# Projections as split float32r products, and a half burst inside a score pair of the attention loop

## The reference, cut to what matters

```python
xn = _layernorm(x)                       # x: 4 x 512 tokens of 256 numbers
q = xn @ Wq.T; k = xn @ Wk.T; v = xn @ Wv.T
scores = jnp.einsum('bsqhd,bthd->bqhst', qh, kh) * scale   # 4 query groups, 8 heads of 8
a_dot = jnp.einsum('bqhst,bthd->bsqhd', jax.nn.softmax(scores), vh)
a_mem = sigma_q @ memory / (sigma_q @ memory_norm)         # sigma_q = elu(q)
out = x + (a_dot * (1 - w) + a_mem * w) + moe(xn)          # moe: shared MLP + 8 experts, top 2
```

## Time and profile before

| what | value |
|---|---|
| median of 3 runs | 735.35 us (734.99 to 736.04) |
| the profiled execution | 736.27 us, of which its span is 734.4 us |
| PE busy | 711.4 us (97%) |
| DVE busy | 577.1 us (79%) |
| ACT busy | 491.1 us (67%) |
| stage 1, up to the first router matmul | 0 to 34.31 us |
| attention, first to last step's first score | 143.3 to 447.5 us |

### The profile page before, as it was taken

How to read it: one execution, slowest core, us unless ns; L and a number is a source line. 1 busy time by engine, 2 the same in 40 slices (tenths; PEclk the granted TensorE clock), 3 DMA queues, 4 the chain that set the end, 5 groups by cost and what they waited for, 6 DMA issues and landing times.

```text
span 734.4 us, 16311 instructions
## 1 busy us (share of the span) xinstructions
PE 711.4 (97%) x5018; PEld 390.0 (53%) x5019; DVE 577.1 (79%) x784; ACT 491.1 (67%) x886; POOL 137.8 (19%) x298
## 2 busy tenths in 40 slices
PE   8999999899999999999999999899999999999998
PEld 3456544622222222222222223688888888888887
DVE  6276488899999999999999982577777878766755
ACT  2472600289999999999999897656566665656332
POOL 1000000666642222111222220100000000005750
PEclk9999999999999999999999999999999999999999
DMA  9829100167521111011111361051111111122431
GB/s 307 283 73 339 51 0 1 34 194 256 181 66 33 33 34 34 30 25 29 33 33 33 117 227 58 16 172 43 57 50 50 50 50 57 43 101 80 136 109 43
DMA packets 50002, 65.41 MB, mean 89 GB/s; under 512 B 8216, under 2 KB 42928, under 8 KB 49968
## 3 DMA queue, kind: packets, MB, share of 16 engines
q1 hardware_dynamic: 37232, 39.92, 17.1%
q10 hardware_dynamic: 9664, 16.66, 6.9%
q0 software_dynamic: 3072, 8.39, 3.6%
HBM read 40.15 MB, written 24.38 MB: 88 GB/s over the span
## 4 chain that ended last, share of the span: by engine, by line
PE 85%; ACT 7%; issue 3%; DVE 3%; POOL 1%; ACTq 1%; DVEq 0%; POOLq 0%
PE ps L1401 16%; PE ps L1432 14%; PE ps L1456 11%; PE ps L1502 9%; PE ps L1279 7%; PE ps L1536 6%; ACT att L752 5%; PE ps L1304 5%; PE ps L1271 3%; PE ps L1551 3%; PE ps L1493 2%; PE ps L1237 2%; ACT o_sb L711 1%; PE ps L1386 1%; PE ps L1414 1%
## 5 line engine op out<-in xcount | busy, mean ns | idle before, releaser
L1025 DVE TENSOR_REDUCE smax<-ps 128x2 f32<-128x1024 f32 x256 | 296.3, 1215 | 20.8 <-PE ps L1304 19.6
L752 ACT ACTIVATE att<-ps 128x512 f32<-128x512 f32 x512 | 274.2, 596 | 32.8 <-PE ps L1456 23.4
L1401 PE MATMUL ps<-att,v_head 128*32 128x256 f32 x2048 | 164.0, 392 | 6.5 <-ACT o_sb L711 6.1
L1456 PE MATMUL ps<-att 51*128 51x512 bf16 x512 | 158.4, 384 | 3.0 <-ACT att L752 1.7
L1304 PE MATMUL ps<-att 48*128 48x512 bf16 x512 | 155.4, 385 | 1.4 <-DVE smax L1025 1.4
L1432 PE MATMUL ps<-att_r 128*128 128x512 f32 x456 | 118.7, 409 | 2.8 <-DVE att_r L1086 2.8
L1082 DVE TENSOR_TENSOR att_r<-big,att_r 128x1024 fp32r<-128x1024 f32 x76 | 89.7, 1221 | 24.2 <-ACT att_r L732 24.2
L1432 PEld LDWEIGHTS ps<-att_r 128*128 128x128 f32 x456 | 86.2, 190 | 21.4 <-DVE att_r L1086 3.3
L1456 PEld LDWEIGHTS ps<-att 51*128 51x128 bf16 x512 | 35.5, 93 | 110.6 <-DVE smax L1025 40.0
L1401 PEld LDWEIGHTS ps<-att,v_head 128*32 128x32 f32 x2048 | 40.5, 108 | 98.2 <-issue 52.5
L732 ACT ACTIVATE att_r<-big 128x1024 fp32r x74 | 74.3, 1052 | 19.0 <-issue 19.0
(11 more groups left out here) (167 smaller groups left out, 702.9 us busy)
## 6 DMA issues: line engine op xcount, KB each, us to landing
big<-w ACTq DMA_DIRECT2D x8, 1024.0 KB
q_stacks<-big SPq DMA_DIRECT2D x12, 512.0 KB
att<-q_stacks SPq DMA_DIRECT2D x64, 96.0 KB
slot_x<-zeros SPq DMA_DIRECT2D x1, 4992.0 KB, 17.1
e_x<-slot_x SPq DMA_DIRECT2D x39, 128.0 KB, 2.0
slot_y<-xn SPq DMA_DIRECT2D x39, 128.0 KB, 1.7
big<-w ACTq DMA_DIRECT2D x8, 512.0 KB
att<-k_stacks SPq DMA_DIRECT2D x64, 48.0 KB
```

Source lines behind the costliest of these rows:

```text
L752: act.activation(probs[:, t % 2, g, :], ps[:, RING[turn_of(u) % 3], :], ACT.Exp, scale=SCALE)\
L1025: dve.reduce_max(smax[:, s % 2, :].rearrange("p (half v) -> p half v", half=2)[:, :, v], ps[:, bank:bank + 2, :], X_AXIS).then_inc(max_don ...
L1401: last = pe.matmul(ps[32 * g:32 * (g + 1), 6, queries], v_head[:, s % 2, t, :], probs[:, t % 2, g, queries], start=s % 2 == 0 and t == 0 a ...
L1456: pe.matmul(ps[:, RING[turn % 3], :], k_st[s][rows, P * t:P * (t + 1)], q_st[s][rows, g, :], start=True, stop=True).then_inc(scores_ready, 1)
```

## The change

In stage 1 each projection becomes three float32r products that are summed in PSUM: high part of the weights times high part of x, low part of the weights times high part of x, and (as `rest`) high part of the weights times low part of x. ACT makes the high parts by copying (the weights once, x from PSUM by `round_xT`), POOL takes the low parts of the weights by two subtractions, DVE those of x by two subtractions a group (`rest_of_xT`). ACT's work is put in another order: one projection result is copied first, then the rounding, then the square root, then the other results, then `copy_xT`. SP waits for the projection weights before it issues the loads of x for groups 2 and 3. Four warm-up matmuls fall away. In stage 3 the half burst that followed pair 2 and the turn of the maxima move into the middle of pair 3, between its two score matmuls; `MAX_AT` goes from 6 to 7 with them, and so does ACT's negation.

```diff
--- before.py
+++ after.py
@@ -154,6 +154,11 @@
         kc = [big[0:DKV, 18432 + 1024 * n:18432 + 1024 * (n + 1)].bitcast(BF16) for n in range(3)]
         wq_sb = big[:, 21504:22016].rearrange("p (k n) -> p k n", k=KD)
         wkv_sb = big[:, 22016:22272].rearrange("p (k n) -> p k n", k=KD)
+
+
+        p_hi, p_lo = [[split[:, 4096 + 2048 * a + 1024 * n:5120 + 2048 * a + 1024 * n]
+                       .rearrange("p (k n) -> p k n", k=KD) for a in range(2)] for n in range(2)]
+        pw_hi, pw_lo = [split[:, 8192 + 768 * n:8960 + 768 * n].rearrange("p (k n) -> p k n", k=KD) for n in range(2)]
         mtmp = big[:, 4096:6144].rearrange("p (a d) -> p a d", a=8)
 
         w1_sb = big[:, 0:16384].rearrange("p (e k n) -> p e k n", e=E, k=KD)
@@ -223,6 +228,10 @@
         xn_ready = sem("xn_ready")
         xT_in_psum = sem("xT_in_psum")
         xT_copied = sem("xT_copied")
+        pw_hi_ready = sem("pw_hi_ready")
+        pw_lo_ready = sem("pw_lo_ready")
+        p_hi_ready = sem("p_hi_ready")
+        p_lo_ready = sem("p_lo_ready")
         lT_in_psum = sem("lT_in_psum")
         lT_copied = sem("lT_copied")
         logits_in_psum = sem("logits_in_psum")
@@ -317,7 +326,7 @@
 
 
         RING = (4, 5, 7)
-        TURNS, MAX_AT, OUT_AT = 18, 6, 13
+        TURNS, MAX_AT, OUT_AT = 18, 7, 13
 
         LAST_OUT = 7
 
@@ -341,7 +350,7 @@
             for j in range(TILES // 2 * 2 - 2, TILES + 2):
                 tile(j, j // 2, j % 2)
 
-        WARM = 18
+        WARM = 14
         FIRST = 2 * NF
         LAST = 2 * NF
 
@@ -359,6 +368,8 @@
             for c in (0, 2):
                 sp.dma_start(acc[:, c, :], x_rows[P * c:P * (c + 1), :]).then_inc(x_first[c], 16)
             for n in range(1, 4):
+                if n == 2:
+                    sp.wait_ge(proj_loaded, 48)
                 sp.dma_start(acc[:, 4 * n:4 * n + 4, :],
                              x_rows[512 * n:512 * (n + 1), :].rearrange("(c p) d -> p c d", p=P))\
                   .then_inc(x_loaded[n - 1], 16)
@@ -517,6 +528,12 @@
                         out=slot_x, out_offset=bass.IndirectOffsetOnAxis(ap=slot[:, n:n + 1], axis=0),
                         in_=xn[:, n % NT, :], in_offset=None).then_inc(scattered, 16)
 
+            pool.wait_ge(pw_hi_ready, 1)
+            pool.tensor_tensor(pw_lo[:, :, 0:2 * P], wq_sb, pw_hi[:, :, 0:2 * P], ALU.subtract)\
+                .then_inc(pw_lo_ready, 1)
+            pool.wait_ge(pw_hi_ready, 2)
+            pool.tensor_tensor(pw_lo[:, :, 2 * P:3 * P], wkv_sb, pw_hi[:, :, 2 * P:3 * P], ALU.subtract)\
+                .then_inc(pw_lo_ready, 1)
             pool.wait_ge(v_copied, 2)
 
             def stage_v(i, b, h, s):
@@ -626,6 +643,7 @@
 
             def copy_xT(n):
                 act.wait_ge(xT_in_psum, n + 1)
+                act.wait_ge(p_lo_ready, n + 1)
                 act.activation(xnT[:, n % 2, 512 * (n // 2):512 * (n // 2 + 1)], ps[:, n % 4, :], ACT.Copy)\
                    .then_inc(xT_copied, 1)
 
@@ -639,15 +657,30 @@
                     ins = act.activation(qf[:, part - 1, 512 * n:512 * (n + 1)], ps[:, 4 + u % 4, :], ACT.Copy)
                 ins.then_inc(qk_copied, 1)
 
+            def round_xT(n):
+
+                act.wait_ge(xT_in_psum, n + 1)
+                if n >= 4:
+                    act.wait_ge(qk_in_psum, 3 * (n // 2 - 1))
+                act.activation(p_hi[n // 2 % 2][:, n % 2, :], ps[:, n % 4, :], ACT.Copy).then_inc(p_hi_ready, 1)
+
             sqrt_var(0)
+            act.wait_ge(proj_loaded, 48)
+            act.activation(pw_hi[:, :, 0:2 * P], wq_sb, ACT.Copy).then_inc(pw_hi_ready, 1)
+            act.activation(pw_hi[:, :, 2 * P:3 * P], wkv_sb, ACT.Copy).then_inc(pw_hi_ready, 1)
             for n in range(4):
+
+                done = range(*UNITS[n - 1]) if n > 0 else ()
+                for u in done[:1]:
+                    copy_qk(u)
+                round_xT(2 * n)
+                round_xT(2 * n + 1)
+                if n < 3:
+                    sqrt_var(n + 1)
+                for u in done[1:]:
+                    copy_qk(u)
                 copy_xT(2 * n)
                 copy_xT(2 * n + 1)
-                if n < 3:
-                    sqrt_var(n + 1)
-                if n > 0:
-                    for u in range(*UNITS[n - 1]):
-                        copy_qk(u)
             for u in range(*UNITS[3]):
                 copy_qk(u)
             act.wait_ge(lT_in_psum, 1)
@@ -868,6 +901,14 @@
                 dve.wait_ge(dve_step, count[0])
 
 
+            def rest_of_xT(n):
+                for m in (2 * n, 2 * n + 1):
+                    dve.wait_ge(p_hi_ready, m + 1)
+                    if n >= 2:
+                        dve.wait_ge(qk_in_psum, 3 * (n - 1))
+                    dve.tensor_tensor(p_lo[n % 2][:, m % 2, :], ps[:, m % 4, :], p_hi[n % 2][:, m % 2, :],
+                                      ALU.subtract).then_inc(p_lo_ready, 1)
+
             for n in range(4):
                 tiles = range(4 * n, 4 * n + 4)
                 part = slice(4 * n, 4 * n + 4)
@@ -882,6 +923,8 @@
                     last = dve.bn_aggr(meanvar[:, c, :], stats[:, c, :])
                 link(last)
                 dve.tensor_scalar_add(meanvar[:, part, 1], meanvar[:, part, 1], EPS).then_inc(var_ready, 1)
+                if n > 0:
+                    rest_of_xT(n - 1)
                 dve.wait_ge(sd_ready, n + 1)
                 link(dve.reciprocal(rstd[:, part], sd[:, part]))
 
@@ -892,6 +935,7 @@
                 for c in tiles:
                     dve.tensor_scalar(xn[:, c, :], acc[:, c, :], meanvar[:, c, 0:1], rstd[:, c:c + 1],
                                       ALU.subtract, ALU.mult).then_inc(xn_ready, 1)
+            rest_of_xT(3)
 
 
             dve.wait_ge(logits_in_psum, 1)
@@ -1224,27 +1268,31 @@
                         if c == 3:
                             ins.then_inc(xT_in_psum, 1)
 
-            def project_qk(u):
+            def project_qk(u, rest):
+
                 n, part = divmod(u, 3)
-                pe.wait_ge(xT_copied, 2 * n + 2)
-                wait(pe, qk_copied, u - 3)
-                for k in range(KD):
-                    tokens = xnT[:, k, 512 * n:512 * (n + 1)]
-                    if part == 0:
-                        last = pe.matmul(ps[:, 4 + u % 4, :], wkv_sb[:, k, :], tokens,
-                                         start=k == 0, stop=k == KD - 1)
-                    else:
-                        last = pe.matmul(ps[:, 4 + u % 4, :], wq_sb[:, k, P * (part - 1):P * part], tokens,
-                                         start=k == 0, stop=k == KD - 1)
-                last.then_inc(qk_in_psum, 1)
+                column = 2 * P if part == 0 else P * (part - 1)
+                if not rest:
+                    pe.wait_ge(p_hi_ready, 2 * n + 2)
+                    wait(pe, qk_copied, u - 3)
+                for ws, xs, w_sem in ((pw_hi, p_lo, pw_hi_ready),) if rest else ((pw_hi, p_hi, pw_hi_ready),
+                                                                                 (pw_lo, p_hi, pw_lo_ready)):
+                    pe.wait_ge(w_sem, 2)
+                    for k in range(KD):
+                        if rest:
+                            pe.wait_ge(p_lo_ready, 2 * n + k + 1)
+                        last = pe.matmul(ps[:, 4 + u % 4, :], ws[:, k, column:column + P], xs[n % 2][:, k, :],
+                                         start=ws is pw_hi and not rest and k == 0, stop=rest and k == KD - 1)
+                if rest:
+                    last.then_inc(qk_in_psum, 1)
 
             for n in range(4):
                 transpose_xn(n)
-                if n == 0:
-                    pe.wait_ge(proj_loaded, 48)
-                for u in range(*UNITS[n]):
-                    project_qk(u)
-
+                for rest in (False, True):
+                    for u in range(*UNITS[n]):
+                        project_qk(u, rest)
+
+            pe.wait_ge(xT_copied, 8)
             pe.wait_ge(router_loaded, 16)
             pe.wait_ge(qk_copied, 9)
             for k in range(KD):
@@ -1459,14 +1507,18 @@
                                 ins = max_scores((s + 2) % 4, v, 1 - half, 2 * (v % 2))
                                 if half == 1:
                                     ins.then_inc(a_ready, 1)
+                            if v == MAX_AT // 2 and half == 0:
+
+                                weighted_values(i, s, 0, 0, pair)
+                                if not last:
+                                    transpose_max(i + 1, s + 1)
                         if t == OUT_AT // G - 1 and g == PAIR - 1 and s % 2 == 0 and not first:
                             transpose_o(pair - 1, (s // 2 + 1) % 2)
                         if t > 0:
-                            weighted_values(i, s, t - 1, g, pair)
+                            if v != MAX_AT // 2 - 1:
+                                weighted_values(i, s, t - 1, g, pair)
                         elif not first:
```

(2 more changed lines are left out.)

## The result

The changed kernel took 743.92 us in the median of 4 runs (741.28 to 746.90), the kernel before 735.69 (4 runs, 734.99 to 736.17): a ratio of 1.0115, with a 95% interval of 1.0083 to 1.0147. The profiled execution took 742.71 us for a span of 741.0, 6.6 above the span of before.

The account below looks back on a forecast made before the run. It took PE, DVE and ACT as all near their limit in attention, and stage 1 as PE nearly alone. Attention +10.8 us and stage 1 -2.7 made +8.1 on the median 735.35: 743.4 us, range 738 to 747.

Parts of the forecast that it names:

- The sum: Whole kernel: attention +10.8 us and stage 1 -2.7, together +8.1 on the median of before.
- Attention: Steps 0 to 29: 15 odd steps lose 0.61 us each, 11 even ones 0.15, together +10.8 us.
- the loop: Attention, new order: from the end of reduction 1 to the start of reduction 3 takes 1.65 us.
- the 0.15: Attention: time from a reduction's end to the start of the score that waited for it, 0.15 us of the 1.65.
- The idle time ahead of reduction 3: Attention: DVE stands idle for 0.6 us there in every step that looks ahead.
- The steps' limits: Attention: ACT's copy holds PE for a third of a microsecond in even steps; DVE holds everything in odd ones.
- the hole is simply filled: Attention rival: score 6 need not wait, even steps gain 0.24 us, odd ones nothing; 729.1 us in all, chance 0.09.
- Stage 1: Projections up to the router's first matmul: DVE sets the pace at 5.68 us a group; gain 2.7 us.
- Attention comes out even: Attention rival: PE and DVE settle at another phase and the wait is absorbed; 732.6 us, chance 0.06.
- Stage 1 gains nothing: Stage 1 rival: late weights or slower DVE subtractions, attention loss as forecast; 745 to 746 us, chance 0.10.
- PE's clock falls in stage 1: Stage 1 rival: PE waiting for DVE meets one lower-clock stretch, costing at most 1.7 us; 745.1 us, chance 0.03.

Follow-up runs that it names:

- e1: The kernel before with the attention edit alone (half burst and turn inside pair 3): 749.37 us, ratio 1.0197.
- e4: The changed kernel, but pair 3's first score goes alone; the wait for reduction 1 and both maxima matmuls follow the turn: 734.25 us, ratio 0.9979.
- e3: The kernel before with only the turn of the maxima moved inside pair 3, the half burst staying after pair 2: 737.84 us, ratio 1.0030.
- e6: The kernel before with the attention edit alone and maxima over 256 of 512 columns: 732.56 us, ratio 0.9951.
- e2: The changed kernel with the old attention loop, so the stage 1 edit alone: 731.91 us, ratio 0.9947 against the kernel before.
- e5: The kernel before with DVE's maxima over 256 of 512 columns: 731.67 us, ratio 0.9934.
- e12: The kernel before with the attention edit, maxima over 256 of 512 columns and ACT's output copy cut to 256 columns: 729.60 us, ratio 0.9915.
- e9: The changed kernel without the third product of each stage 1 projection: one execution, 742.66 us, router's first matmul at 29.43.
- e8: The changed kernel without SP's wait for the projection weights ahead of the x loads of groups 2 and 3: 747.66 us, ratio 1.0158.
- e7: e1 with ACT's loads of late experts spread one, one and two over steps 28 to 30: 748.23 us, ratio 1.0151.
- e11: The changed kernel with ACT's copy of the output cut to 256 of 512 columns: 743.72 us, ratio 1.0113.
- e10: The kernel before with ACT's copy of the output cut to 256 of 512 columns: 732.01 us, ratio 0.9951.

## Why the prediction came out as it did

**The sum.** +8.1 was forecast; the medians differ by 8.2. The executions with a mean clock of 1.000 differ less: 741.28 (one run) against 733.65 (one of 23 runs of before beside e1 to e4), 7.6. Part of the agreement of the medians is luck: the terms were off in both directions by some tenths of a microsecond (below), and both medians hold falls of the clock that the sum does not have.

**Attention.** The step that carried it, that everything behind score 6 waits for reduction 1, is shown by e3, e4 and e6. The sizes: the loop came out at 1.57 us instead of 1.65. The mis-sized term is the 0.15 from a reduction to the score that waited for it. Inside the hardware loop of steps 4 to 27 it is 0.06 (304.63 to 304.69); only the unrolled steps 0 to 3, 28 and 29 have the 0.15. I had read it at another score of the odd step of before (311.21), and took that score to wait for DVE. Its row has no bracket, and 0.06 after the reduction's end would have been 311.12: something else held it. The idle time ahead of reduction 3 came out as 0.44 us instead of 0.6: 0.08 of that is the shorter loop, and 0.09 a slip, since the 1.13 from which I took the overlap of two reductions already had it taken off. Odd steps lost 0.55 instead of 0.61; even ones 0.04 and 0.18 in turn, 0.11 in the mean, instead of 0.15. The total of +9.1 for 10.8 is lower still, since before's profile had a fall of the clock in step 0, which took 10.6 us there. Against e2, which has the old loop and no fall in attention (303.2 us from the first score of step 0 to that of the last step), the 313.4 of the changed kernel are 10.2 longer.

**The steps' limits** are where my reading was incomplete, and the number did not show it. I wrote that DVE holds everything in odd steps; e5, whose reductions take 0.69 us instead of 1.22, has odd steps only 0.07 shorter, so another limit stood right behind it. Then the even step. I held that PE is held there by ACT's copy for a third of a microsecond, and priced the rival *the hole is simply filled* at 0.24 us a step, 729.1 in all. e6 removes what I argued against it, DVE, and gains nothing, and e12 beside it shows that the hole isn't PE's to fill: ACT sets the step, and the rival would have given nothing in attention, leaving about e2's 731.9.

**Stage 1.** A gain of 3.1 for 2.7. DVE sets the pace, as the sum had it (e9); a group takes 5.42 us instead of 5.68, because the subtractions overlap both the addition before them and the reciprocal behind them. The two subtractions took 1.28 for the estimated 1.29, and 12 float32r records run from 10.54 to the next line's first at 13.39, 0.238 us each for 0.229. Three groups give 0.8 us and their earlier start 0.2, of which 0.7 was lost again behind the last group, from its transposes at 24.42 to 31.19, 6.8 instead of 6.1.

**The rivals.** *Attention comes out even*: out, odd steps kept none of their time. *Stage 1 gains nothing*: out here, but e8 shows how near it was, one wait on SP away. *PE's clock falls in stage 1*: not in the changed kernel, but it is what happened in e8, with 1.5 us for the first products, near the 1.7 I had as its bound.

## What to carry to other kernels

Before an instruction is moved to fill an idle engine, list what it waits for, since all that follows it on its queue inherits that wait; here a hole of 0.36 us in every second step was paid for with 0.55 in the others. An idle gap names the wait that ended last, not the engine that sets the period: to find that one, shorten the suspected work (here a copy, by 0.2 us) and see if the period follows. Two edits of one change should be timed apart: one of these was worth -3.6 us, and together they cost 8.

## What the runs showed of the hardware

Times of one and the same kernel go with the mean granted clock of the execution: the kernel before took 733.65 us at 1.000, 735.0 to 735.6 at 0.998, 738.4 to 739.0 at 0.993 and 740.85 at 0.988. I had counted such a fall once, in stage 1. The kernels in which PE waits for DVE in attention (the changed kernel, e1, e7, e8 and e11) had a mean of 0.995 or less in 17 of 22 executions, the kernel before in 21 of 52, e3 in 5 of 9, and the other kernels (e2, e4, e5, e6, e10 and e12) in 5 of 49. In the rows above the falls come behind stretches in which PE stood idle for a good part: busy 1.83 of 3.40 and 2.99 of 4.50 us, where it waited for an exponential behind ACT's issues, and 0.00 of 3.38, where it waited for the late weights. The Trainium skill (TensorE: Matmul & The Clock Gate, "HAM oscillation") tells of such falls where bursts of matmuls are parted by waits for transfers; the row of e8 agrees, and in the other two the wait was for ACT. A schedule that leaves PE a little sparser may so lose more than its own waits: e1's steps 4 to 27 lost 7.3 us, its median 13.8. That the waits for DVE, and not the loads alone, bring on the longer falls is argued from these counts, not shown.
